# Gate and up products of a two-layer hybrid block as three float32r matmuls of high and low parts

## What is computed

```python
h = silu(x @ w_gate) * (x @ w_up)        # x after layernorm, 256 -> 1024
h_sparse = _sparsify_2to4(h)             # of each 4 neighbours the 2 largest by magnitude
return h_sparse @ w_down                 # 1024 -> 256

x = x + attn_a(layernorm(x));  x = x + ffn(layernorm(x))
x = x + attn_b(layernorm(x));  x = x + ffn(layernorm(x))
```

## Time and profile of the kernel before

| | us |
|---|---|
| time, median of 3 runs | 1692.22 |
| lowest and highest | 1691.9, 1693.53 |
| span of the profiled execution | 1690.8 |
| PE busy | 1649.8 (98%) |
| DVE busy | 1470.8 (87%) |
| ACT busy | 1281.1 (76%) |
| POOL busy | 267.9 (16%) |

### The profile page before, as it was taken

How to read it: one execution, slowest core, us unless ns; L and a number is a source line. 1 busy time by engine, 2 the same in 40 slices (tenths; PEclk the granted TensorE clock), 3 DMA queues, 4 the chain that set the end, 5 groups by cost and what they waited for, 6 DMA issues and landing times.

```text
span 1690.8 us, 39058 instructions
## 1 busy us (share of the span) xinstructions
PE 1649.8 (98%) x13872; PEld 651.3 (39%) x13872; DVE 1470.8 (87%) x2144; ACT 1281.1 (76%) x2424; POOL 267.9 (16%) x623
## 2 busy tenths in 40 slices
PE   6899999999999999999988999999999999999999
PEld 4322222222222224776653222222222222257777
DVE  6999999999999993675668999999999999837655
ACT  3399999999999997333124999999999999963320
POOL 1410000000000000000012223333223333310000
PEclk9999999999999999999998999999999999999999
DMA  6943343333453311100404322222232222121000
GB/s 172 290 89 63 74 83 62 72 76 65 83 149 62 73 47 54 50 1 0 115 14 130 68 60 50 50 64 56 52 72 57 50 63 57 43 64 31 13 13 25
DMA packets 72124, 114.67 MB, mean 68 GB/s; under 512 B 12464, under 2 KB 27824, under 8 KB 71984
## 3 DMA queue, kind: packets, MB, share of 16 engines
q1 hardware_dynamic: 71984, 112.63, 28.8%
HBM read 71.96 MB, written 40.63 MB: 67 GB/s over the span
## 4 chain that ended last, share of the span: by engine, by line
PE 94%; DVE 3%; DMA 1%; issue 1%; ACT 1%; SPq 0%; POOLq 0%; DVEq 0%; ACTq 0%
PE psum L762 34%; PE psum L744 21%; PE psum L820 13%; PE psum L714 13%; PE psum L842 6%; PE psum L677 2%; PE psum L800 2%; DVE mneg L1236 1%; PE psum L697 1%; PE psum L659 1%; PE psum L732 1%; DMA area<-k_stacks 0%; DVE xn L1242 0%; DVE area L1286 0%; ACT xnT L959 0%
## 5 line engine op out<-in xcount | busy, mean ns | idle before, releaser
L1008 ACT ACTIVATE area<-psum 128x512 f32<-128x512 f32 x2048 | 1097.3, 600 | 39.8 <-PE psum L744 11.9
L762 PE MATMUL psum<-area 128*32 128x256 f32 x8192 | 655.1, 392 | 0.4 <-POOL area L1491 0.4
L744 PE MATMUL psum<-area 51*128 51x512 bf16 x2048 | 639.4, 386 | 2.5 <-DVE vsb L1186 1.4
L1242 DVE CUSTOM_DVE_ANT_0 xn<-psum,band 128x1024 f32<-128x1024 f32 x512 | 588.3, 1220 | 10.3 <-PE psum L714 9.1
L1236 DVE TENSOR_REDUCE mneg<-psum 128x1 f32<-128x1024 f32 x512 | 581.0, 1217 | 7.0 <-PE psum L714 6.9
L762 PEld LDWEIGHTS psum<-area 128*32 128x32 f32 x8192 | 162.0, 108 | 400.4 <-issue 258.8
L714 PE MATMUL psum<-area 48*128 48x512 bf16 x1024 | 301.1, 386 | 7.9 <-DVE mneg L1236 4.6
L744 PEld LDWEIGHTS psum<-area 51*128 51x128 bf16 x2048 | 141.4, 94 | 426.8 <-ACT area L1008 354.2
L714 PE MATMUL psum<-k_max_b,area 48*128 48x512 bf16 x1024 | 292.9, 385 | 5.3 <-DVE mneg L1242 4.7
L1053 ACT ACTIVATE area<-psum 128x512 f32<-128x512 f32 x64 | 38.2, 597 | 161.5 <-PE psum L820 161.5
L1472 POOL TENSOR_TENSOR mparts<-mneg,nought 128x16 bf16<-128x16 f32 x64 | 14.2, 222 | 741.2 <-DVE mneg L1236 500.4
(11 more groups left out here) (74 smaller groups left out, 823.6 us busy)
## 6 DMA issues: line engine op xcount, KB each, us to landing
ctx_rows<-area SPq DMA_DIRECT2D x64, 256.0 KB, 2.1
area<-q_stacks SPq DMA_DIRECT2D x32, 384.0 KB, 6.9
area<-k_stacks SPq DMA_DIRECT2D x64, 192.0 KB, 5.5
area<-q_stacks_b SPq DMA_DIRECT2D x32, 384.0 KB, 5.3
area<-q_stacks SPq DMA_DIRECT2D x32, 192.0 KB, 4.6
area<-q_stacks_b SPq DMA_DIRECT2D x32, 192.0 KB, 3.6
area<-ctx_rows SPq DMA_DIRECT2D x16, 256.0 KB, 4.0
area<-inv_rows SPq DMA_DIRECT2D x16, 256.0 KB, 4.5
```

Source lines behind the costliest of these rows:

```text
L744: pe.matmul(psum[:, BANK_OF["exp", g, u, head], :], k_st[lo:lo + ROWS + PARTS, buf, 0 if a else head // 2, kt * P:(kt + 1) * P], q_st[lo:l ...
L762: mm = pe.matmul(psum[head * VW:(head + 1) * VW, BANK_OF["ctx", g, qh], cols], vaug[:, buf, kt, head, :], probs[:, u % PRING, head, cols], ...
L1008: act.activation(probs[:, u % PRING, head, :], psum[:, BANK_OF["exp", like, u, head], :], ACT.Exp, scale=SCALE).then_inc(bank_freed, 1)
L1242: dve.tensor_tensor_reduce(band_out[:, c % 2, :], slot, band[:, at:at + SEQ], 1.0, -3.0e38, ALU.add, ALU.max, mneg[:, qh, col:col + 1]).th ...
```

## The change

**Products.** Each normed chunk is kept as two float32r tensors: `xd_hi` is the copy that ACT makes (`copy_transposed` now writes it for odd `k`), and `xd_lo` is what is left, PSUM minus `xd_hi`, by two new DVE instructions for each chunk (`residue`, 512 elements each). The weights are four tensors, `wg_hi`, `wg_lo`, `wu_hi`, `wu_lo`, with the columns of one `r` next to each other. A gate or an up product of one `r` is now six matmuls: `w_hi` and `w_lo` with `xd_hi`, and `w_hi` with `xd_lo`, each over two `k`.

**Weights.** The DMAs put `w_gate` and `w_up` as they are into the space of `xnT`. `split_dense_weights` on DVE, once, behind `invert_sums(0, 0)`, makes four `tensor_copy` of 1024 elements (read with a step of four, cast to float32r) and four subtractions.

**Space.** `wg_hi` and `wg_lo` lie over `vsb_a`, the chunks' parts over `xnT`, `q_st` and `sums`.

```diff
-        wg = sb("wg", [P, DK, INNER])
-        wu = sb("wu", [P, DK, INNER])
+        wu_hi = sb("wu_hi", [P, DK, INNER // P, P], F32R)
+        wu_lo = sb("wu_lo", [P, DK, INNER // P, P], F32R)
...
             def gate_up(f, c, h, leading=(), rows=range(4)):
 
                 pe.wait_ge(ln_evac, 2 * (4 * (2 * f + 1) + c) + 2)
+                if f == 0 and c == 0 and h == 0:
+                    pe.wait_ge(whole_split, 2 * DK)
+                pair = ((wg_hi, wg_lo, 0, gate_ready), (wu_hi, wu_lo, 2, up_ready))
+
+                def times_high(w_hi, w_lo, to, r):
+                    for part in (w_hi, w_lo):
+                        for k in range(DK):
+                            pe.matmul(to, part[:, k, 4 * h + r, :], xd_hi[c][:, k, :],
+                                      start=(part is w_hi and k == 0), stop=False)
+
+                def times_low(w_hi, to, r, done):
+                    for k in range(DK):
+                        mm = pe.matmul(to, w_hi[:, k, 4 * h + r, :], xd_lo[c][:, k, :], start=False,
+                                       stop=(k == DK - 1))
+                    mm.then_inc(done, 1)
+
                 for r in rows:
                     n = 32 * f + 8 * c + 4 * h + r
...
+                    if n >= 2:
+                        pe.wait_ge(hid_done, n - 1)
+                    if r == 0 and h == 0:
+                        for w_hi, w_lo, base, done in pair:
+                            if c == 0 and base == 2:
+                                pe.wait_ge(xd_split, 2 * (4 * f + c) + 2)
+                            times_high(w_hi, w_lo, psum[:, base + r % 2, :], r)
+                        pe.wait_ge(xd_split, 2 * (4 * f + c) + 2)
+                        for w_hi, w_lo, base, done in pair:
+                            times_low(w_hi, psum[:, base + r % 2, :], r, done)
+                    else:
+                        for w_hi, w_lo, base, done in pair:
+                            times_high(w_hi, w_lo, psum[:, base + r % 2, :], r)
+                            times_low(w_hi, psum[:, base + r % 2, :], r, done)
...
                 if c == 1:
-                    pe.wait_ge(ln_evac, 2 * (4 * (2 * f + 1) + 3) + 2)
+                    pe.wait_ge(xd_split, 2 * (4 * f + 3) + 2)
...
                 gate_up(a, 0, 1)
-                pe.wait_ge(ln_evac, 2 * (4 * (2 * a + 1) + 1) + 2)
+                pe.wait_ge(xd_split, 2 * (4 * a + 1) + 2)
                 project_out(a, 2)
...
+            def residue(k, c):
+
+                for tp in range(2):
+                    dve.wait_ge(ln_evac, 2 * (4 * k + c) + tp + 1)
+                    cols = slice(2 * tp * P, (2 * tp + 2) * P)
+                    dve.tensor_tensor(xd_lo[c][:, :, cols].rearrange("p d (t c) -> p d t c", t=2),
+                                      psum[:, turned_banks(k, c)[tp], :].rearrange("p (t d c) -> p d t c", t=2, d=DK),
+                                      xd_hi[c][:, :, cols].bitcast(F32).rearrange("p d (t c) -> p d t c", t=2),
+                                      ALU.subtract).then_inc(xd_split, 1)
+
+            def split_dense_weights():
+                dve.wait_ge(wf_loaded, 48)
+                dve.wait_ge(vaug_ready, GROUPS)
+                pairs = [(w_raw[i][:, k, :].rearrange("p (h c r) -> p h r c", h=2, r=4),
+                          hi[:, k].rearrange("p (h r) c -> p h r c", h=2),
+                          lo[:, k].rearrange("p (h r) c -> p h r c", h=2))
+                         for i, (hi, lo) in enumerate(((wg_hi, wg_lo), (wu_hi, wu_lo))) for k in range(DK)]
+                for whole, hi, lo in pairs:
+                    dve.tensor_copy(hi, whole).then_inc(whole_hi, 1)
+                for n, (whole, hi, lo) in enumerate(pairs):
+                    dve.wait_ge(whole_hi, n + 1)
+                    dve.tensor_tensor(lo, whole, hi.bitcast(F32), ALU.subtract).then_inc(whole_split, 1)
...
                 invert_sums(a, 0)
+                if a == 0:
+                    split_dense_weights()
                 divide_ctx(a, 0)
...
                 add_attention(a, 1)
+                residue(2 * a + 1, 0)
                 norm(2 * a + 1, 1)
                 invert_sums(a, 1)
                 hidden(a, 0, 0, follower=(0, 1))
+                residue(2 * a + 1, 1)
                 divide_ctx(a, 2)
...
-                hidden(a, 1, 1, follower=(2, 0))
+                hidden(a, 1, 1, follower=(2, 0), turned=(2 * a + 1, 2))
+                residue(2 * a + 1, 3)
```

More of the change, by code:

```diff
@@ L21 @@
 BF16 = mybir.dt.bfloat16
+F32R = mybir.dt.float32r
 ALU = mybir.AluOpType
@@ L270, in hybrid_kernel, with over @@
                  + [parts_mid[:, i] for i in range(2)] + [parts_top[:, 0], parts_far[:, 0]])
+        def over(name, at, shape):
+            return nc.alloc_sbuf_tensor_at(name, shape, F32R, offset=at)
+        wg_hi = over("wg_hi", vsb_at, [P, DK, INNER // P, P])
+        wg_lo = over("wg_lo", vsb_at + 4 * DK * INNER, [P, DK, INNER // P, P])
+        CHUNK_BYTES = 4 * DK * BANK
+        xd_at = [(xnT_at, xnT_at + CHUNK_BYTES),
+                 (area_at + 4 * q_st_at, area_at + 4 * q_st_at + CHUNK_BYTES),
+                 (area_at + 4 * q_st_at + 3 * CHUNK_BYTES, sums_at),
+                 (xnT_at + 2 * CHUNK_BYTES, xnT_at + 3 * CHUNK_BYTES)]
+        xd_hi = [over(f"xd_hi{c}", at, [P, DK, BANK]) for c, (at, _) in enumerate(xd_at)]
+        xd_lo = [over(f"xd_lo{c}", at, [P, DK, BANK]) for c, (_, at) in enumerate(xd_at)]
+        w_raw = [xnT[:, 2 * i:2 * i + 2].rearrange("p c k t -> p (c k t)").rearrange("p (k n) -> p k n", k=DK)
+                 for i in range(2)]
         def xn_of(k, c):
@@ L956, in copy_transposed @@
                 n = 4 * k + c
+                if k == 1 and c == 0:
+                    act.wait_ge(whole_split, 2 * DK)
                 for tp in range(2):
                     act.wait_ge(ln_tr, 2 * n + tp + 1)
-                    act.copy(xnT[:, :, (c * CT + 2 * tp) * P:(c * CT + 2 * tp + 2) * P].rearrange(
-                        "p d (t c) -> p d t c", t=2),
+                    to = xd_hi[c] if k % 2 else xnT[:, c]
+                    act.copy(to[:, :, 2 * tp * P:(2 * tp + 2) * P].rearrange("p d (t c) -> p d t c", t=2),
                         psum[:, turned_banks(k, c)[tp], :].rearrange("p (t d c) -> p d t c", t=2, d=DK)
@@ L1271, in gated_product, with hidden @@
                                   ALU.mult).then_inc(hid_done, 1)
-            def hidden(f, c, h, follower=None, begun=0, leading=(), between=(), splits=(), scaled=()):
+            def hidden(f, c, h, follower=None, begun=0, leading=(), between=(), splits=(), scaled=(), turned=()):
                 n0 = 8 * f + 2 * c + h
@@ L1287, in hidden @@
                                       mag[:, lo + 1:4, :], ALU.is_ge).then_inc(wins_done, 1)
+                    if turned and lo == 0:
+                        residue(*turned)
                 dve.wait_ge(wins_done, 3 * (n0 + 1))
```

34 lines of the change are left out of this document (16 added, 18 removed).

## The result

The changed kernel takes 1661.78 us (1660.23 to 1661.84, four runs) against 1692.88 us for the kernel before beside it (1691.9 to 1693.59): a ratio of 0.9815, 95% interval 0.9801 to 0.9829. The forecast was 1657.7 us, in a range of 1641 to 1676. Of the 34.5 us forecast, 31.1 came. The profiled execution has a span of 1659.8 us, 31.0 less than before.

A forecast was written before the change was run, and what follows sets the result against it. PE was taken to bound the kernel, until DVE is late. Products save 54.0 us, 37.7 after waits; less 3.2 for clock, 34.5 off 1690.8 gives a 1656.3 span, 1657.7 us with 1.4 for the median; range 1641 to 1676.

The forecast's parts named there:

- new clock falls: PE's clock dropping after a new 3.0 us wait, once a dense stage: 3.2 us lost, bounds 0 and 2 x 3.5.
- the old clock fall: After PE's existing 2.84 us idle, windows mostly at 1.2 GHz, 1.6 us lost; the basis for pricing later drops.
- the split: Eight DVE weight instructions, 7.5 to 9.4 us from 634.5, covered by DVE's idle time, costing nothing.
- Price of a matmul: Gate and up products on PE: 215.8 ns per float32r matmul, from L842's record; 54.0 us of PE time saved.
- Rival 3: Float32r products on PE: weight loads not hidden, 322 ns or more a matmul, kernel slower, near 1720 or 1782; chance 0.11.
- The new waits: PE waiting for DVE in the dense stages: 8.2 us lost in the second stage, 8.1 in the first.
- the ledger: Walk through each dense stage's PE and DVE times: gains of 18.8 and 18.9 us after waits, 37.7 together.
- The first stage's entries: First dense stage: the two first second-stage losses (1.5, 3.0), then 1.0, 1.9 and 0.9; written sum 8.1 us.
- The waits of the last three halves: Halves 6 to 8 in a row: DVE's 11.1 us against PE's 10.4, late follower products, 2.5 us lost.
- the old wait for `rest`: First dense stage: the two existing PE waits for `rest` move along unchanged.
- rival 2: Weight split late (4.3 us, up to 10), longer waits, or clock losses at more places: 1662 to 1674 us; chance 0.16.
- DVE near the bound: Sign of being right: DVE close to limiting the last three halves, its half 11.1 us against PE's 10.4.

## Why the prediction was right, point by point

The direction, the mechanism and the range were right. That the sum came out only 3.5 us off is in good part luck, because its terms missed in opposite ways. From the 34.5 us forecast: products 13.0 less, waits 9.0 more, no new clock falls 3.2 more, the old clock fall gone 1.7 more, the split 1.3 less, later maxima 1.0 less, small places 2.1 less; that leaves 31.0.

- **Price of a matmul, mis-sized.** 215.8 ns was taken, 233 measured: 54.0 us of PE time became 41.0. The row of L842 that I went by has the columns, the load and the gaplessness right, but it is of float32, whose passes take 0.42 ns a column; nothing in the trace showed float32r's 0.449. The prediction gave bounds, 213 and 858 ns, but its sum had only the one value. The trace shows one record for each matmul, at about the time of one stream of its columns. The Trainium skill ("FP8 and Floating Point Precision", TensorE Precision Notes) gives true float32 four passes and reduced float32 no such number; the trace agrees, with 233 ns against 858.
- **Rival 3, weight loads not hidden, is out.** The loads of 188 ns lie inside a spacing of 233, and where they were recorded at 205 the spacing was 118. The rule of the Trainium skill ("TensorE: Matmul & The Clock Gate", Part 3, The mechanism) that a load overlaps a running matmul only in another row group does not fit these rows taken alone, in which all matmuls use all rows; the same section also names loads into a background weight buffer, and no run here tells whether that is what hides them.
- **The new waits, mis-sized the other way.** 16.3 us in the ledger, 7.3 measured. (The first stage's entries add up to 8.3, not to the 8.1 written there.) Every place of it that it gave over a us to showed, with its cause: 0.87 for 1.5 before n = 2, 1.74 for 3.0 before the projection of chunk 2 in both stages, 1.58 for 1.9 before `scale(2, 0)`. They shrank because PE came later than I had it: by 0.2 us an n. In the bfloat16 kernel, where PE has my price, the wait is 2.58. The waits of the last three halves (2.5) came to 0.5 as recorded, and to 1.3 by the time that these halves took.
- **PE's clock, mis-sized.** It was to fall after the new wait in both stages, 3.2 us; at 1.74 us it did not in either, so the term came to nothing. In the bfloat16 kernel, with 2.6 us in both stages, it fell in the first and stayed at 1.00 in the second; in the kernel with half the weight load it fell behind 1.89 us in the first (5.38 us for the projection) and stayed behind as long a wait in the second (3.69). What decides it stays open. That the old wait for `rest` would keep its clock fall was wrong too, by 1.7 us in the kernel's favour.
- **The split** was taken as free; it cost 1.3 us. The step of four made all of them longer, casts from 0.6 to 1.0 us and the two-input subtractions 1.75 times. That is rival 2's mechanism, at a third of its price, since casts without the step are cheaper than the 1.17 us in the sum. The Trainium skill ("SBUF — State Buffer", Door 1: The DMA port swizzle), whose rule that each step to a new 16-byte line pays speaks against the step, was right in kind.
- **DVE near the bound**: borne out in the last three halves, 34.9 us where PE alone would take 33.5, against DVE's floor of 11.8 us a half; and with half of the stream taken away PE gained 88 us and the kernel 14.6. DVE's 35% of the whole chain does not show it, as most of that is attention a.

## What to carry to other kernels

Before pricing a new form of instruction from a neighbour's row, keep the type apart from the size: here the same columns cost 215 or 233 ns by type. When the busiest engine needs a fifth less time for its products, list what its partner puts ahead of each thing that it waits for, since the order that was free before is not any more; here reordering and moving 12 us of DVE work gave 6 us, and a matmul faster by 18 ns gave 1.4 us alone (one run, with a clock fall in it) and 6.3 us behind the reordering. Work that is moved to an idle POOL must not run beside DVE instructions with two SBUF inputs; here that cost 9.6 us. Before an effect of 2 us is read from single runs, compare PE's granted clock behind its waits.

## What the runs showed of the hardware that I had not expected

- A float32r matmul of 128x128 by 512 columns stands 233 ns from the next, of 256 columns 118; bfloat16 215 at 512.
- A recorded load of 205 ns does not keep matmuls from standing 118 ns apart.
- On DVE a read with a step of four floats costs 1.0 instead of 0.6 us in a cast of 1024 and 2.0 instead of 1.14 in a subtraction of 1024.
- POOL's subtractions stopped a DVE divide with two SBUF inputs for 9 us, over four POOL instructions; maxima read from PSUM were not slowed beside POOL's casts and subtractions.
- PE's clock falls or stays after one and the same wait of 2.5 us, 1.7 us apart where it fell in the kernel without the step.
